# Causal attention of a four-layer model: query blocks in another order, chunks prepared while scores run, the diagonal bias of half the heads through ScalarE and GpSimd

## The reference, cut to what matters

```python
q = heads(x @ Wq + bq); k = heads(x @ Wk + bk); v = heads(x @ Wv + bv)   # 16 heads of 8
q = q * cos + rotate_half(q) * sin
k = k * cos + rotate_half(k) * sin
bias = rel_bias_table[bucket(pos_q - pos_k)]       # one bucket for all distances from 128 on
att = (einsum('bhid,bhjd->bhij', q, k) + bias) * (1 / sqrt(8))
att = where(pos_k <= pos_q, att, -inf)             # causal
y = einsum('bhij,bhjd->bhid', softmax(att), v)
return y @ Wp + bp
```

## Time and profile before

| | us |
|---|---|
| median of 3 runs (3899.31 to 3905.27) | 3900.71 |
| the profiled execution, its own time | 3900.87 |
| its span, first to last instruction | 3899.0 |
| attention stage of layer 3, in the trace | 2957 to 3644 |

### The profile page before, as it was taken

How to read it: one execution, slowest core, us unless ns; L and a number is a source line. 1 busy time by engine, 2 the same in 40 slices (tenths; PEclk the granted TensorE clock), 3 DMA queues, 4 the chain that set the end, 5 groups by cost and what they waited for, 6 DMA issues and landing times.

```text
span 3899.0 us, 56360 instructions
## 1 busy us (share of the span) xinstructions
PE 3394.0 (87%) x22347; PEld 1736.5 (45%) x22353; DVE 2716.3 (70%) x5773; ACT 1817.1 (47%) x3210; POOL 893.0 (23%) x702
## 2 busy tenths in 40 slices
PE   2679875699979999999979988888997999999899
PEld 2322222465652333333346666656774233233576
DVE  7787868787759999999477773454435887673433
ACT  1232221377755777777667773223222245545321
POOL 0235542377720000000086660000302000000000
PEclk8879877799998999999989998988999799899999
DMA  0000000211100000000031100001100000000100
GB/s 20 9 0 1 1 0 0 67 31 38 31 8 1 1 1 1 1 1 1 1 85 29 34 23 23 6 23 46 44 1 28 1 1 1 1 1 1 45 1 12
DMA packets 48255, 60.19 MB, mean 15 GB/s; under 512 B 9268, under 2 KB 34232, under 8 KB 47608
## 3 DMA queue, kind: packets, MB, share of 16 engines
q1 hardware_dynamic: 47992, 56.59, 5.3%
HBM read 39.22 MB, written 1.10 MB: 10 GB/s over the span
## 4 chain that ended last, share of the span: by engine, by line


## 5 line engine op out<-in xcount | busy, mean ns | idle before, releaser
L142 PE MATMUL ps<-AR 128*128 128x128 f32 (+12 forms) x17304 | 2204.8, 427 | 154.1 <-DVE AR L114 42.3
L131 ACT ACTIVATE AR<-ps 128x1024 f32<-128x1024 f32 (+6 forms) x1720 | 1265.6, 778 | 1195.6 <-PE ps L142 951.8
L142 PEld LDWEIGHTS ps<-AR 128*32 128x32 f32 (+8 forms) x17304 | 1058.4, 149 | 1335.9 <-DVE AR L125 404.0
L125 DVE TENSOR_REDUCE AR<-ps 128x1 f32<-128x512 f32 (+1 forms) x1424 | 935.6, 709 | 84.6 <-PE ps L142 83.9
L114 POOL TENSOR_TENSOR rs<-rs,halves 128x4 f32<-128x4 f32 x68 | 71.1, 1046 | 2470.1 <-DVE rs L118 2469.3
L131 ACT ACTIVATE AR<-ps,AR 128x128 f32<-128x128 f32 (+1 forms) x764 | 402.5, 544 | 390.4 <-PE ps L142 362.6
L114 POOL TENSOR_TENSOR AR<-AR 128x512 f32<-128x512 f32 (+4 forms) x348 | 466.7, 1356 | 311.4 <-DVE AR L114 193.9
L142 PE MATMUL ps<-XT,AR 128*128 128x512 f32 x896 | 427.1, 612 | 2.5 <-DMA AR<-in_L3f_w 2.3
L114 DVE TENSOR_TENSOR AR<-ps,AR 128x512 f32<-128x512 f32 (+3 forms) x626 | 300.4, 528 | 135.7 <-PE ps L142 96.9
L122 DVE SCALAR_TENSOR_TENSOR X<-ps,AR,X 128x128 f32<-128x128 f32 x512 | 143.8, 344 | 343.6 <-PE ps L142 343.3
L150 PE MATMUL ps<-C,AR 128*128 128x128 f32 x1593 | 246.4, 292 | 135.2 <-ACT AR L131 60.0
(11 more groups left out here) (85 smaller groups left out, 1850.3 us busy)
## 6 DMA issues: line engine op xcount, KB each, us to landing
AR<-AR SPq DMA_DIRECT2D x124, 128.0 KB, 2.3
AR<-in_c_rot SPq DMA_DIRECT2D x64, 128.0 KB, 2.3
AR<-in_L3f_w SPq DMA_DIRECT2D x32, 256.0 KB, 5.8
AR<-in_L2f_w SPq DMA_DIRECT2D x32, 128.0 KB, 2.8
AR<-scr_bias SPq DMA_DIRECT2D x32, 128.0 KB, 3.1
WR<-in_c_rot SPq DMA_DIRECT2D x1, 2048.0 KB, 8.8
WR<-in_L_ffn_wqkv SPq DMA_DIRECT2D x2, 768.0 KB
AR<-in_L_ffn_wqkv SPq DMA_DIRECT2D x2, 768.0 KB
```

Source lines behind the costliest of these rows:

```text
L125: return self.do(lambda e: e.tensor_reduce(o, a, AXX, op, negate=neg, apply_absolute_value=mag), *w)
L131: return self.do(lambda e: e.activation(o, a, f, bias=bias, scale=scale, accum_out=acc), *w)
L142: last = e.matmul(o, l, r, start=a, stop=z, skip_group_check=True)
```

## The change

The order of the blocks becomes 0, 1, 2, 3 for groups 0 and 2 and 3, 2, 1, 0 for groups 1 and 3. Only chunk 0 is prepared ahead; all else that was done ahead of the loop goes to a list `background`, of which a step takes one entry, or more where `need` finds a missing piece. The DVE half of a spread is queued at the start of the next step. The product form of the bias is gone: for heads 0 and 1 of a near step ACT copies the near columns to SBUF, POOL adds the table, ACT takes the exponential of the sum, and the far columns have an exponential of their own. The table `BF` now has all sixteen heads: 16 calls of `table_step`, 8 with three products, from expert 3 on.

```diff
@@ attn8
-        HB0, BF, BN, thb = g.near_bias
+        BF, BN, thb = g.near_bias
+        NB = ar.f32(2, 2, 256)
+        nbf, nnb = [None, None], [0]
-        antib = ar.bf16(128)
-        V.copy(antib, g.anti)
...
-    tT = turn(g, g.XN, g.XT, tn)
+    tT = {} if causal else dict(enumerate(turn(g, g.XN, g.XT, tn)))
+
+    def turn_in(c, b):
+        t = P.tr([(g.bank[b][:, 128 * k:128 * k + 128], g.XN[:, 4 * c + k, :]) for k in range(4)],
+                 g.ident, g.free[b], tn[4 * c:4 * c + 4])
+        g.free[b] = tT[c] = A.act(g.XT[:, 512 * c:512 * c + 512], g.bank[b], ACT.Copy, t)
...
+    def spread_step(gr, c, k):
+        return lambda: later.append(spread(gr, c, k, spare()))
+
+    def value_rows(i):
+        return lambda: project_v(i)
+
+    def chunk_steps(c, banks):
+        def some(k):
+            return banks[k] if banks else spare()
+        return [lambda: turn_in(c, some(0)), lambda: compact(c, 1, some(1), some(2)), lambda: compact(c, 0, some(3), some(0))]
+
+    def flush():
+        while later:
+            spread_low(*later.pop(0))
+
+    def need(table, key):
+        while key not in table:
+            if later:
+                flush()
+            else:
+                background.pop(0)()
...
-    stages = [(gr, qc) for gr in range(4) for qc in ((3, 2, 1, 0) if gr % 2 == 0 else (0, 1, 2, 3))]
+    stages = [(gr, qc) for gr in range(4) for qc in ((0, 1, 2, 3) if (gr % 2 == 0) == causal else (3, 2, 1, 0))]
@@ max_pair
+        need(tsp, (gr, qc, 0))
+        need(tsp, (gr, kc, 1))
@@ score_pair
-                          QK[32 * h:32 * h + 32, 0, s, 512 * qc + lo:512 * qc + 512], True, u == 1 or not near))
+                          QK[32 * h:32 * h + 32, 0, s, 512 * qc + lo:512 * qc + 512], True, True))
-    def bias_by_products(n, kt):
-        gr, qc = stages[n]
-        a, z = near_cols(n, kt)
-        return P.mm([(g.bank[k][:, a - 512 * qc:z - 512 * qc], antib,
-                      HB0[:, m, bias_index(gr, k), a - 128 * kt:z - 128 * kt], False, m == 2)
-                     for k in range(2) for m in range(3)], thb)
...
+    def exp_near(n, kt, t):
+
+        gr, qc = stages[n]
+        a, z = near_cols(n, kt)
+        y, w, x = nnb[0] % 2, z - a, 2 * kt % 4
+        nnb[0] += 1
+        src = g.ps[:, 0:1024].rearrange("p (a b) -> p a b", a=2)
+        dst = PB[:, x, :].rearrange("p (a b) -> p a b", a=2)
+        lo, hi = a - 512 * qc, z - 512 * qc
+        nb = NB[:, y, :, 0:w]
+        tc = A.act(nb, src[:, :, lo:hi], ACT.Copy, t, nbf[y])
+        free = [tc]
+        tp = G.tt(nb, nb, BF[:, 4 * gr:4 * gr + 2, a - 128 * kt:z - 128 * kt], ALU.add, tc, thb)
+        if hi < 512:
+            free.append(A.act(dst[:, :, hi:512], src[:, :, hi:512], ACT.Exp, t, pbf[x], scale=scale))
+        g.free[0] = g.free[1] = free
+
+        def last():
+            te[n, kt, 0] = nbf[y] = A.act(dst[:, :, lo:hi], nb, ACT.Exp, tp, pbf[x], scale=scale)
+        return last
@@ value_step
+        need(tvv, kt)
@@ step_products
+        need(tsp, (stages[n][0], kt // 4, 1))
         if order:
             max_reduce(max_pair(*order.pop(0)))
         t0 = score_pair(n, kt, 0)
         t1 = score_pair(n, kt, 1)
         if near:
             t1 = bias_by_adding(n, kt, t1)
-        for k in range(2 if near else len(order)):
-            if order:
-                max_reduce(max_pair(*order.pop(0)))
+            last = exp_near(n, kt, t0)
+        else:
+            exp_pair(n, kt, 0, t0)
+        exp_pair(n, kt, 1, t1)
         if near:
-            t0 = bias_by_products(n, kt)
-        exp_pair(n, kt, 0, t0)
-        exp_pair(n, kt, 1, t1)
+            last()
         for x in order:
             max_reduce(max_pair(*x))
@@ ahead of the loop
+    if causal:
+        for step in chunk_steps(0, (0, 1, 2, 3)):
+            step()
+        background.extend(spread_step(0, 0, k) for k in (1, 0))
+        for c in range(1, 4):
+            background.extend(chunk_steps(c, None))
+            background.extend(spread_step(0, c, k) for k in (1, 0))
+            background.extend(value_rows(i) for i in range(4 * c - 4, 4 * c))
+        background.extend(value_rows(i) for i in range(12, 16))
+        background.extend(spread_step(1, c, 1) for c in range(4))
+        background.extend(spread_step(1, c, 0) for c in (3, 2, 1, 0))
...
-    goal = target(0.0)
+    goal = full[0] + 1e-6 if causal else target(0.0)
@@ the loop over steps
+        flush()
         step_products(n, kt, target(p + area[j]))
...
-        elif extra:
-            spread_low(*spread(*extra.pop(0), spare()))
+        elif background:
+            background.pop(0)()
@@ near_bias
-        G.copy(HB0[:, 0], HB[:, 0:8], tl)
-        tl = G.copy(HB1[:, 0], HB[:, 8:16])
-        for m in (1, 2):
-            t2 = [G.tt(HB[:, 0:8], HB[:, 0:8], HB0[:, m - 1], ALU.subtract, tl),
-                  G.tt(HB[:, 8:16], HB[:, 8:16], HB1[:, m - 1], ALU.subtract)]
-            tl = [G.copy(HB0[:, m], HB[:, 0:8], t2), G.copy(HB1[:, m], HB[:, 8:16])]
-        made.extend([tr, tl])
+        tl = load_bias(0, None)
+        made.append(G.copy(antib, g.anti))
+        made.append(G.fill(BN[:, :, 0:384], 0.0))
+        made.append(G.copy(HR, HB, tl))
+        tl = G.copy(HP[:, 0], HB, load_bias(1, made[2]))
+        tl = G.tt(HB, HB, HP[:, 0], ALU.subtract, tl)
+        tl = G.copy(HP[:, 1], HB, tl)
+        made.append(G.tt(HP[:, 2], HB, HP[:, 1], ALU.subtract, tl))
@@ moe
-            if bias_steps and 4 <= e < 7:
-                bias_steps[1](4 * e + c - 16, 4 + (4 * e + c + 2) % 4)
+            if bias_steps and 3 <= e < 7:
+                bias_steps[1](4 * e + c - 12, 4 + (4 * e + c + 2) % 4)
```

More of the change, by code:

```diff
@@ L1188, in attn8 @@
     PB = ar.f32(4, 1024)
-    assert not causal or ar.at <= 41500 - 10240
+    assert not causal or ar.at <= 41500 - 9216
     tmn = G.fill(MN.rearrange("p a b c -> p (a b c)"), 0.0)
@@ L1275, in max_pair @@
                        MQK[32 * h:32 * h + 32, 1, s, 512 * kc:512 * kc + w], True, True)],
-                     g.free[b], tsp[gr, qc, 0], [tsp[gr, c, 1] for c in range((512 * kc + w + 511) // 512)])
+                     g.free[b], tsp[gr, qc, 0], tsp[gr, kc, 1])
             o = 384 + 512 * kc - 128 * (i - 1)
-            bias = BN[:, bias_index(gr, h), o:o + w] if near else None
+            bias = BN[:, 4 * gr + h, o:o + w] if near else None
             out.append((n, h, st, kc, w, b, bias, t))
@@ L1331, in bias_by_adding @@
         x = g.ps[:, 1024:2048].rearrange("p (a b) -> p a b", a=2)[:, :, a - 512 * qc:z - 512 * qc]
[L1332 removed]
+        return V.tt(x, x, BF[:, 4 * gr + 2:4 * gr + 4, a - 128 * kt:z - 128 * kt], ALU.add, t, thb)
+    def exp_near(n, kt, t):
[16 more added lines that the diff above has]
+        return last
     def exp_pair(n, kt, u, t):
@@ L1434, in attn8 @@
     V.fill(g.bank[O], 0.0, g.free[O])
     g.free[O] = V.now()
-    for c in range(5):
-        if c >= 1:
-            for k in range(2):
-                half_done.append(spread(0, c - 1, k, 5 + k))
-        if c < 4:
-            for k in range(2):
-                compact(c, k)
-        while half_done:
-            spread_low(*half_done.pop(0))
-    for i in range(NT):
-        project_v(i)
-    todo = [(gr, c, k) for gr in range(1, slots) for c in range(4) for k in (1, 0)]
-    ne = 0
-    goal = target(0.0)
@@ L1450, in attn8 @@
-    while todo or half_done or upto[min(done)] <= goal:
+    if causal:
[9 more added lines that the diff above has]
+        background.extend(spread_step(1, c, 0) for c in (3, 2, 1, 0))
+    else:
+        for c in range(5):
+            if c >= 1:
+                for k in range(2):
+                    later.append(spread(0, c - 1, k, 5 + k))
+            if c < 4:
+                for k in range(2):
+                    compact(c, k, 2 * k, None)
+            flush()
+        for i in range(NT):
+            project_v(i)
+        background.extend(spread_step(gr, c, k) for gr in range(1, slots) for c in range(4) for k in (1, 0))
@@ L1451, in attn8 @@
+    goal = full[0] + 1e-6 if causal else target(0.0)
+    while (background and not causal) or upto[min(done)] <= goal:
         for half in (1, 0):
-            was, half_done = half_done, []
+            was = later[:]
+            del later[:]
             for x in next_pairs(half, goal, 1):
@@ L1480, in attn8 @@
                 if slots == 2 and pn % 4 == 3 and stages[pn][0] + 2 < 4:
-                    extra += [(stages[pn][0] + 2, c, k) for c in range(4) for k in (1, 0)]
+                    up = (0, 1, 2, 3) if stages[pn][0] % 2 == 0 else (3, 2, 1, 0)
+                    background.extend(spread_step(stages[pn][0] + 2, c, k) for c in up for k in (1, 0))
         p += area[j]
@@ L1579, in l2_attn @@
         settled(g, c, g.free[b])
-def bias_index(gr, h):
-    return 8 * (h // 2) + 2 * gr + h % 2
 def near_bias(g):
@@ L1588, in near_bias @@
     top = Arena(g.ar.t, 41500)
-    top.at = 41500 - 10240 - 7168
+    top.at = 41500 - 9216 - 10240
```

(13 more changed lines are left out.)

39 lines of the change are left out of this document (16 added, 23 removed).

## The result

The changed kernel is slower: 3963.7 us (median of 4 runs, 3957.0 to 3965.2) against 3903.0 for the kernel before on the same chip, ratio 1.0153 (95% interval 1.0135 to 1.017). The forecast was 3850, range 3815 to 3893. The profiled execution has a span of 3962.4 us.

The account below looks back on a forecast made before the run. TensorE, busy 87%, was taken as the main load, with VectorE setting layer 3's opening and first stages. From 3900.9 us, -54 (opening), -3 (loop, bias gain included) and +4 (table) gave 3848, rounded to 3850; range 3815 to 3893.

Parts of the forecast that it names:

- The slower one: Rival: layer 3's first three stages run PE at 1.2 GHz, 226 us instead of 124, +102, 3952; chance 0.08.
- Part 1: Layer 3's attention, diagonal steps: bias of heads 0 and 1 off PE saves 2.6 us a stage, 42 us in all.
- the walk: Step-by-step timing along a layer 3 block's diagonal without maxima: 15.4 us where it was 16.4 + 1.6.
- ACT's four in a row: Layer 3's diagonal steps: four ScalarE instructions in sequence (0.60 + 0.60 + 1.02 + 0.60 us) set the step.
- Part 2: Opening of layer 3's attention: first exponential after 42 us in place of 96, -54 us; bounds 39 and 62.
- Part 3: Layer 3's attention loop: 574 us against 577, -3 us; bias gain paid back by moved maxima, chunks and spreads.
- the prediction's own cuts: Layer 3's stages are cut at their first exponential; the first three were forecast at 124 us.
- the chains that `need` forces: Layer 3's first three stages: turn, product, rotation, spread in series; for these DVE's share taken as 0.855, giving 124 us.
- over 150 us in the first three stages: Layer 3's loop: a stated sign of the prediction being wrong, set against 124 us forecast there.
- Part 4: Feed-forward stage ahead of layer 3's attention: the table for all heads costs +4 us, bounds 2 and 6.

Follow-up runs that it names:

- fixed: Also written (1): changed kernel with layer 1's 24 spreads back on banks 0 to 3 in turn; 3898.0 us, ratio 0.9986.
- (6): fixed, with all of layer 3's chunks, group 0's spreads and value rows prepared ahead of the loop; 3883.4 us, ratio 0.995.
- (11): Kernel before with the bias part alone, plus VectorE adding the bias of heads 0 and 1 in the last four stages; 3890.4 us, ratio 0.9968.
- (5): fixed, with the bias of heads 0 and 1 back in PE's products and the old table; 3906.8 us, ratio 1.0002.
- (9): (7), with the bias of heads 0 and 1 back in PE's products and the old table; 3879.2 us, ratio 0.9939.
- (7): (6), with group 1's eight spreads in layer 3 on banks 0 to 3 instead of the ring of banks 5 to 7; 3870.3 us, ratio 0.991.
- (2): Kernel before, with layer 1's 24 spreads taking their bank from the ring of banks 5 to 7; 3966.7 us, ratio 1.0155.

## Why the prediction was wrong

**The step that failed is the scope.** The prediction says "What is edited is one stage of twelve, 2957 to 3644, and a table made in the stage before it", and its sum has no term for layer 1. The measured term is +63 us. Without it the result would be no change that can be told (fixed is 0.14% faster), so the sizes below were off as well, by 48 us together. The whole diff showed the edit, though its excerpt above does not: the line `half_done.append(spread(*todo.pop(0), ne % 4))` goes, and what takes its place serves both branches. I read `causal` branches as "layer 3 alone" and did not walk the other branch line by line. A check was at hand: the number of banks that each loop's spreads may take, four before and one in effect after.

**The rivals.** The slower one, 3952, came closest in its number, by luck: it put the loss, +102 us over the forecast, in layer 3's first stages by the clock. These took 36 over it, and the loss lies in layer 1. Its reading of the earlier trace rows was off too: PE is busy 17.28 of 18 us there, at 0.50, and no waiting shows in that row. In layer 3's first stages the clock was 0.68, 0.82 and 0.87, and (6) took 44 us out of these stages at no higher clock (0.63, 0.75, 0.88), so the clock alone does not set them. It may well be a part of the 36: PE was busy 129 us of 160 where the prediction counted 113 at full clock, and no run raised the clock in these stages. The clock of 0.50 in layer 1 comes with the waiting and goes with it (1), and costs some 27 us of the rounds by the estimate above. The Trainium skill, "TensorE: Matmul & The Clock Gate", "A second HAM failure mode: psum-queue depth-cycling", tells of a kernel that cycles through PSUM banks, in which PE idles for short whiles so often that its clock swings between the two levels. Layer 1's rounds agree in part: each has a gap on PE of 2.03 us, but their spreads stay on one bank, and the clock does not swing, it is 0.50 throughout.

**Part 1, bias (-42): half right.** Measured alone -18.4 in the attention. A diagonal without maxima fell from 18.0 to 15.0 us (forecast 15.4), so the walk's length held where it was made; its limit, ACT's four in a row, is not the only one (11). It was applied to all sixteen stages alike: blocks 1 to 3 gave 2.1 each on average, and block 0 cost 1.0 each. Why block 0 loses stays open: its steps are small for copy, add and two exponentials in a row, but it did not gain when (11) took them away. 4 x 3.6 and 12 x 0.5, 20 us, are most of what is missing.

**Part 2, opening (-54): mis-sized by 7.** 49.4 us to the first exponential instead of 42 (46.0 in fixed). The 63.0 to the first value product hold 13 us of what the prediction counts to stage 0. In the first 50 us DVE is busy 24 (10.5 and 13.3 in the rows of after), and the clock is 0.57: the 3 us put down for PE's waits on the chain were too few.

**Part 3, the loop (-3): its first three stages are the largest wrong size, 36 us.** By the prediction's own cuts they took 159.8 us and not 124 (159.5 in fixed). DVE's busy time was near (115.8 against 106), its share was not: 0.72, against the 0.855 taken for "the chains that `need` forces"; with the chains ahead of the loop it was 0.86 (6). From 3092 to 3243 PE waited 9.6 us for the spreads' and the rotation's instructions on DVE (L122) and 2.7 for POOL's adds, so the chains are part of the 36. How much is theirs, how much the ring's, which the spreads in the loop share with the maxima, and how much the clock's, stays open. Stages 3 to 15 took 453 (forecast 450), though the bias part gave less than the forecast had put in it, so that some other price of the sum there was too high; which one stays open. I stated over 150 us in the first three stages as a sign of being wrong, and it showed.

**Part 4, the table (+4): right as far as can be told.** 4.1 us in seven kernels with the new table, 5.5 and 5.7 in fixed and after. But the stage took 1.6 and 1.8 more in (5) and (9) too, which have the old table, so the table itself costs some 2 to 4 us.

With the measured sizes and without layer 1 the sum is even: -9.1 in layer 3, +5.7 in the feed-forward, and the fixed kernel at 3898. The order's gain at the start was real (38 us) and was given back in the loop. What was worth having in it shows in (7): few maxima ahead of the first score, but the chains ahead of the loop, and four banks for them.

## What to carry to other kernels

When a helper's buffers move from one pool to another, count the banks that each user may hold at once: a ring of three, shared by a pair and a single, gives the single always the same bank. Walk every caller and every branch of a function that the diff touches, above all the branch that is not the change's aim. Ask of work moved "into the background" what forces it: here the chains through PE, ACT, DVE and POOL that a step must finish cost more inside the dense loop than ahead of it (opening and stages 0 to 2 took 209 us with them in the loop, 202 ahead of it, 188 ahead with four banks).

## What the runs showed that was not expected

One choice of PSUM bank for 24 products was worth 65 us of 3902, eight times what can be told from no change, and the page hardly shows it. The engines' row of (2), the kernel before with that edit alone, against the earlier trace rows: DVE and ACT the same, PE 16 us more.

```profile
PE 3409.6 (86%) x22347; PEld 1739.2 (44%) x22353; DVE 2720.5 (69%) x5773; ACT 1817.0 (46%) x3210; POOL 897.7 (23%) x702
```

What a low granted clock costs depends on where PE stands. In layer 1's rounds PE, at 0.50, takes turns with DVE, and nothing hides that its fp32 products take 1140 ns in the mean where they took 645. In layer 3 extra products raised it in two stretches of the opening, from 0.73 to 0.83 and from 0.50 to 0.67, and the stage did not get shorter; their own time may have eaten the gain.
